# Causal mask of transposed attention scores: one 128x128 matmul per head in place of two 64x64 ones

## The chip, the cores and the metric
The kernel runs on one core of one Trainium2 chip. The metric is device time in microseconds (us) of one execution. Lower is better. TensorE, the matrix engine, appears in the profile as PE (matmuls) and PEld (loading of the stationary operand). VectorE is DVE, ScalarE is ACT, GpSimd is POOL and SyncE, which issues transfers, is SP.

## The reference, cut to what matters
The network has two layers. The first is a state space mixer with a dense mixture of experts, the second is causal self-attention with a routed mixture of experts. The change lies in the attention of the second layer, which has 4 sequences of 512 tokens, 16 heads, and 8 numbers per head:

```
q = apply_rope((x @ W_q.T).reshape(B, S, H, dk).transpose(0, 2, 1, 3))
k = apply_rope((x @ W_k.T).reshape(B, S, H, dk).transpose(0, 2, 1, 3))
v = (x @ W_v.T).reshape(B, S, H, dk).transpose(0, 2, 1, 3)
scores = jnp.einsum('bhqd,bhkd->bhqk', q, k) / sqrt(dk)
scores = jnp.where(jnp.tril(jnp.ones((S, S), dtype=bool)), scores, -jnp.inf)
probs = jax.nn.softmax(scores, axis=-1)
attn = jnp.einsum('bhqk,bhkd->bhqd', probs, v)
```

A query sees only keys at its own position or before it. Of each 128x128 tile on the diagonal, the half with keys behind the query is masked.

## The kernel before, in words
Attention is done in 16 groups of four heads: group s is sequence b = s // 4, heads 4(s % 4) to 4(s % 4) + 3. One pass of the loop `for it in range(-2, 17)` (line 1719) handles three groups at different stages, in eight slots i = 0 to 7. The order of TensorE's work is written out by hand in this loop, and the other engines have loops of the same form. In one slot TensorE does:

- `scores(it + 2, u)` (line 1628, its matmul is recorded under L1641): scores of the group two ahead with queries as rows, into one of three PSUM banks that are used in turn (`RING = 3`, function `ring_bank`). DVE takes the maximum of each row from there (L1221) and so frees the bank. A head's operand has 48 rows (q and k each split in bf16 pieces) and lies in partitions 0 to 47 or 64 to 111, by the head's parity. Slots 0, 2 and 4 hold work of an even head alone, 1, 3 and 5 of an odd head alone, 6 and 7 of both.
- `scores_T(8 * it + i)` (line 1655): one unit of transposed scores of the present group, keys as rows, for two heads, hh = 0 in partitions 0 to 63 and hh = 1 in partitions 64 to 127. First the mask is written to the unit's two banks (L1667), then the scores are accumulated over it (L1672, 51 rows: 48 and three that subtract the row's maximum). It waits for `probs` of the unit two before. The key tile is 3 for slots 0 and 1, then 2, 1 and 0, so that the score matmul has 128, 256, 384 and 512 columns.
- In odd slots `weighted_values` (L1686, fp32, output of 32 columns per head), which waits for `probs`; in slot 2 `maxima_T` (L1651); in slot 3 `o_T` (L1695); in some passes `a_T` (L1702), `attn_out` (L1710), projections of q and k (L1599) and of v (L1624).

ACT computes the exponentials of a unit from its two banks (`probs`, L778). POOL splits the finished maxima in bf16 pieces (`max_parts`, L522 to L528) before `maxima_T` can transpose them. There are 128 units in all. Passes it = 14 and 15 have no `scores`.

In the listings a matmul's shape is written rows*columns of the stationary operand, then that of the moving one: `64*128 64x64` is 64 rows and 128 output partitions with 64 columns streamed.

The mask operand comes from `shape_constants` and is loaded once, in the bf16 constant pack.

Of the kernel before, what the change touches and what calls it, by code (L numbers as in the profile page):

```python
# [13 lines left out]
P = 128  # L14
# [14 lines left out]
HALF = 64  # L29
# [4 lines left out]
NEG = -1e30  # L34
# [19 lines left out]
    "const": [("ident", 128), ("tri", 128), ("after", 128), ("cos", 512), ("sin", 512), ("iota", 8),  # L54
              ("mask", 512), ("segment", NT * E1), ("full", NT), ("block", NBLK), ("number", NT), ("spare", NBLK)],
}
BPACK = [("identb", 128), ("causal", 256), ("half", 64)]


def offsets(fields):  # L60
    out, at = {}, 0
    for name, width in fields:
        out[name] = (at, at + width)
        at += width
    return out, at


def adaln_kernel(nc, x_in, mod_in, mixw_in, moe0_in, attn_in, moe1_in, const_in, bconst_in, kones_in, out):
    with ExitStack() as ctx:
        def sb(name, shape, dt=F32):  # L70
            return ctx.enter_context(nc.sbuf_tensor(name, shape, dt))
# [3 lines left out]
        def sem(name):  # L75
            if name not in sems:
                sems[name] = ctx.enter_context(nc.semaphore(name))
            return sems[name]

        ps = ctx.enter_context(nc.psum_tensor("ps", [P, 8, 512], F32))  # L80

        w = {}
        packed = {}
        for pack, fields in PACKS.items():
# [4 lines left out]
            for name, (lo, hi) in off.items():  # L89
                w[name] = t[:, lo:hi]  # L90
        off, total = offsets(BPACK)
        bconst = sb("bconst", [P, total], BF16)
        for name, (lo, hi) in off.items():
            w[name] = bconst[:, lo:hi]
        ident, identb = w["ident"], w["identb"]
# [1241 lines left out]
        def _(pe):  # L1337
            pe.wait_ge(sem("siluc"), 1)
            for c in range(6):
                for layer in range(2):  # L1340
                    mm = pe.matmul(ps[:, 0, (2 * c + layer) * B:(2 * c + layer + 1) * B],
                                   w[f"wmod{layer}"][:, c * D:(c + 1) * D], siluc[:, layer * B:(layer + 1) * B],
                                   start=True, stop=True)
# [4 lines left out]
            for b in range(B):  # L1348
                for n, c in enumerate((0, 1, 2)):
                    mm = pe.matmul(ps[:, 1 + b, n * D:(n + 1) * D], modT[:, c, 0, b:b + 1].to_broadcast([P, P]), ident,  # L1350
                                   start=True, stop=True)
                mm.then_inc(sem("mod0_ps"), 1)
            for b in range(B):
                if b == 3:
                    pe.wait_ge(sem("mod0"), 1)
                for n, c in enumerate((2, 3, 4, 5)):
                    mm = pe.matmul(ps[:, MOD1_BANK[b], n * D:(n + 1) * D], modT[:, c, 1, b:b + 1].to_broadcast([P, P]),
                                   ident, start=True, stop=True)
# [69 lines left out]
            for i in range(NT + 3):  # L1428
                if i < NT:

                    t, k = i, i % 2
                    tok = slice(t * P, (t + 1) * P)
                    pe.wait_ge(sem("ua"), HEADS * (t + 1))
                    if t >= 2:
                        pe.wait_ge(sem("L"), t - 1)
                    pe.matmul(ps[:, k, :], w["after"], ua[:, k].rearrange("p h s -> p (h s)"), start=True,
                              stop=True).then_inc(sem("seg_ps"), 1)
                    if t >= 1:
# [3 lines left out]
                              stop=True).then_inc(sem("g_ps"), 1)  # L1442
                if i < 2:
                    to_tokens(B - 2 + i)
                if 0 <= i - 2 < NT:
                    t, k = i - 2, i % 2
# [9 lines left out]
                if 0 <= i - 1 < NT:  # L1456

                    t, k = i - 1, (i - 1) % 2
                    c, b = t % TPB, t // TPB
                    tok = slice(t * P, (t + 1) * P)  # L1460
                    if c < TPB - 1:
                        pe.wait_ge(sem("Xd"), t + 1)
                        if t >= 1:
                            pe.wait_ge(sem("prev"), 3 * b + c)
                        pe.matmul(ps[:, 5, k * DI:(k + 1) * DI], Bt[:, t, :], Xd[:, k].rearrange("p h e -> p (h e)"),
                                  start=True, stop=True).then_inc(sem("state_ps"), 1)
# [11 lines left out]
                    for hh in range(HEADS):  # L1478
                        mm = pe.matmul(ps[:, 3 + k, hh * HP:(hh + 1) * HP], M[:, k, hh, :], X[:, k, hh, :],
                                       start=True, stop=True)  # L1480
                    mm.then_inc(sem("y_ps"), 1)
                if 0 <= i - 3:
                    t, k = i - 3, (i - 3) % 2
# [6 lines left out]
                    for q in range(2):  # L1490
                        mm = pe.matmul(ps[:, 7, P * (1 + k):P * (2 + k)], yT[:, k, q, :], wor[:, q, :],
                                       start=(q == 0), stop=(q == 1))
# [80 lines left out]
            for i in range(32):  # L1573
                e = i % E0
                pe.wait_ge(sem("xm"), i + 1)
                if i >= 2:
# [3 lines left out]
                          stop=True).then_inc(sem("p1_ps"), 1)  # L1580
                pe.matmul(ps[:, 4 + i % 2, :], w["w3"][:, e * D:(e + 1) * D], xm[:, i % 2, :], start=True,  # L1581
                          stop=True).then_inc(sem("p3_ps"), 1)
# [72 lines left out]
            def scores_T(u):  # L1655
                s, i = divmod(u, 8)
                b, g = divmod(s, QG)
                kt, jp = 3 - i // 2, i % 2
                n = S - kt * P
                if i == 0:  # L1660
                    pe.wait_ge(sem(f"m_rows{s % 2}"), 64 * (s // 2 + 1))
                if u >= 2:
                    pe.wait_ge(sem("probs"), u - 1)
                for qh in range(2):
                    for hh in range(2):
                        bank, lo = 4 + 2 * (u % 2) + hh, HALF * hh
                        pe.matmul(ps[:, bank, HALF * qh:HALF * (qh + 1)],  # L1667
                                  w["causal"][lo:lo + HALF, qh * P:(qh + 1) * P], w["half"][lo:lo + HALF, :],
                                  start=(qh == 0), stop=True, skip_group_check=True)
                for hh in range(2):  # L1670
                    bank, lo = 4 + 2 * (u % 2) + hh, HALF * hh
                    mm = pe.matmul(ps[:, bank, 0:n], kaug[lo:lo + KM, b % 2, 2 * g + jp, kt * P:(kt + 1) * P],  # L1672
                                   qaug[lo:lo + KM, b % 2, 2 * g + jp, kt * P:S], start=False, stop=True,
                                   skip_group_check=True)
                mm.then_inc(sem("st_ps"), 1)
# [43 lines left out]
            for it in range(-2, 17):  # L1719
                if it == -1:  # L1720
                    transposes(3, 2, bank=4)
                    transposes(3, 3, bank=4)
                for i in range(8):
                    if it + 2 < 16:
                        for u in at_slot[i]:
                            scores(it + 2, u)
                    if 0 <= it < 16:
                        scores_T(8 * it + i)
                    if i % 2 == 1 and 0 <= 4 * it + i // 2 - 1 < 64:
                        weighted_values(4 * it + i // 2 - 1)  # L1730
                    if i == 2 and 0 <= it + 1 < 16:
                        maxima_T(it + 1)
                    if i == 3 and 0 <= it - 1:
                        o_T(it - 1)
                    if i == 5 and it >= 4 and it % 4 == 0:
                        a_T(it // 4 - 1)
                    if i == 7 and it >= 4 and it % 4 == 0:
                        attn_out(it // 4 - 1)
                    for b, j in ropes_at(it, i):
                        project(b, j)  # L1740
                    if it in (4, 8) and i == 6:
                        project_values((it + 4) // 4)
# [45 lines left out]
def shape_constants():  # L1788
    import numpy as np

    k = np.arange(P)
    pos = np.arange(S, dtype=np.float32)
    inv = np.float32(10000.0) ** (-np.arange(0, DK, 2, dtype=np.float32) / np.float32(DK))
    ang = (pos[:, None] * inv[None, :]).astype(np.float32)
    d = np.arange(P) % DK
    cos = np.cos(ang)[:, d // 2].T
    sin = np.sin(ang)[:, d // 2].T * np.where(d % 2 == 0, -1.0, 1.0)[:, None]
    mask = np.zeros((P, 4 * P), np.float32)
    mask[:, 3 * P:4 * P] = np.where(k[None, :] > k[:, None], NEG, 0.0)
    const = {  # L1800
        "ident": np.eye(P), "tri": k[:, None] <= k[None, :], "after": k[:, None] > k[None, :],
        "cos": cos, "sin": sin, "iota": np.broadcast_to(8.0 - np.arange(8), (P, 8)), "mask": mask,
        "segment": np.broadcast_to(np.arange(NT * E1) % NT > 0, (P, NT * E1)),
        "full": np.broadcast_to(P * np.arange(NT), (P, NT)),
        "block": np.broadcast_to(np.arange(NBLK), (P, NBLK)),
        "number": 1 + k[:, None] + P * np.arange(NT)[None, :],
        "spare": 1 + NTOK + k[:, None] + P * np.arange(NBLK)[None, :],
    }
    bconst = {
        "identb": np.eye(P),  # L1810
        "causal": np.concatenate([np.where(k[None, :] > k[:, None] % HALF + HALF * qh, NEG, 0.0) for qh in range(2)],
                                 axis=1),
        "half": k[:, None] % HALF == np.arange(HALF)[None, :],
    }
    fc = np.concatenate([np.asarray(const[n], np.float32) for n, _ in PACKS["const"]], axis=1)
    bc = np.concatenate([np.asarray(bconst[n], np.float32) for n, _ in BPACK], axis=1).astype(np.dtype("bfloat16"))
    kones = np.full((3, NH // 2, S), -1.0, np.float32)
    return fc, bc, kones.astype(np.dtype("bfloat16"))


def lay_out(i):
# [41 lines left out]
    }  # L1863
    packs["x_in"] = np.ascontiguousarray(a["L0_attn_x"].reshape(NT, P, D).transpose(1, 0, 2))
    packs["const_in"], packs["bconst_in"], packs["kones_in"] = shape_constants()
    return packs

# [14 lines left out]
```

## Time and profile before

| | |
|---|---|
| median of 3 timed runs | 580.0 us (579.58 to 580.09) |
| the profiled execution's own time | 577.07 us |
| its span in the trace | 575.2 us |
| mean granted TensorE clock | 0.889 of full |
| PE busy, DVE busy, ACT busy, POOL busy | 452.4, 392.0, 278.1, 271.6 us |
| attention loop, from the first L1667 to the last | 313.9 to 460.2 us |
| L1667, the mask matmuls | 512 matmuls, 45.6 us busy, 195 ns mean |
| L1672, the transposed scores | 256 matmuls, 52.2 us busy, 307 ns mean |

A span is the time from the first to the last instruction in the trace. The 1.9 us between it and the execution's own time lie around it. Busy time of an engine is the union of its instructions' durations. The duration of a matmul includes its way through the array, which overlaps with the next matmul. So what a matmul costs in a stream is the distance from its start to the start of the next, not its duration.

### The profile page before, as it was taken

The numbers are of one execution on the slowest core, as the hardware profiler recorded it, in microseconds if no ns is written. First come the engines' busy times: TensorE is split into PE (matmuls) and PEld (weight loads), VectorE is DVE, ScalarE is ACT, GpSimd is POOL, SyncE is SP. The second block draws the span as 40 slices with busy tenths as digits, with TensorE's granted clock in tenths as the row PEclk, the third lists the DMA queues.
The fourth block names the chain that finished last, engine by engine and source line by source line (L and its number), as shares of the span: only waits on it lengthen the run. The fifth ranks groups of instructions, "written<-read, shape, count | busy, mean of one in ns | idle before, by whom it ended". The sixth has DMA issues, their size and how long they took to land.

```text
span 575.2 us, 10088 instructions
## 1 busy us (share of the span) xinstructions
PE 452.4 (79%) x3120; PEld 274.4 (48%) x3120; DVE 392.0 (68%) x1264; ACT 278.1 (48%) x518; POOL 271.6 (47%) x392
## 2 busy tenths in 40 slices
PE   3688778987998999994558998999999863059970
PEld 3545456766653444442323434435445343049970
DVE  5789738988655888886679687888898235025533
ACT  1568796653453544441223577678777831013220
POOL 4210038998301786664641047476655502714541
PEclk9988889999799999997775799999999985559995
DMA  8600000000335333310386012222300000141114
GB/s 354 169 1 1 0 2 2 1 2 1 144 148 125 99 106 99 107 62 2 108 208 124 4 31 88 82 86 85 84 5 4 3 0 10 52 123 36 36 38 146
DMA packets 25739, 39.94 MB, mean 69 GB/s; under 512 B 3228, under 2 KB 17756, under 8 KB 25164
## 3 DMA queue, kind: packets, MB, share of 16 engines
q1 hardware_dynamic: 21752, 30.42, 17.8%
q0 software_dynamic: 3936, 8.89, 5.2%
q8 instruction: 26, 0.43, 0.3%
q14 instruction: 25, 0.20, 0.1%
HBM read 27.55 MB, written 11.55 MB: 68 GB/s over the span
## 4 chain that ended last, share of the span: by engine, by line
PE 49%; DVE 18%; POOL 11%; issue 8%; ACT 6%; DMA 6%; SPq 0%; DVEq 0%; POOLq 0%; ACTq 0%
PE ps L1579 5%; PE ps L1581 5%; PE ps L1568 5%; PE ps L1686 4%; PE ps L1599 3%; PE ps L1771 3%; PE ps L1782 3%; POOL slots_x L586 3%; DVE rows L406 3%; PE ps L1391 2%; DVE moe L1221 2%; PE ps L1641 2%; POOL qk_parts L305 2%; DVE st L387 2%; PE ps L1672 2%
## 5 line engine op out<-in xcount | busy, mean ns | idle before, releaser
L1221 DVE CUSTOM_DVE_ANT_0 moe<-ps,const 128x512 bf16<-128x512 f32 (+3 forms) x256 | 110.5, 486 | 9.7 <-PE ps L1641 9.4
L778 ACT ACTIVATE arena<-ps 128x256 f32<-128x256 f32 (+3 forms) x128 | 85.8, 701 | 33.6 <-PE ps L1672 32.9
L476 POOL TENSOR_TENSOR arena<-arena 128x512 f32<-128x512 f32 x32 | 51.7, 1616 | 51.9 <-DVE arena L1139 51.7
L1641 PE MATMUL ps<-arena 48*128 48x128 bf16 (+3 forms) x256 | 56.1, 329 | 10.7 <-DVE arena L1221 4.7
L1672 PE MATMUL ps<-arena 51*128 51x128 bf16 (+3 forms) x256 | 52.2, 307 | 0.0
L1686 PE MATMUL ps<-arena 128*32 128x512 f32 (+3 forms) x512 | 48.4, 450 | 0.9 <-ACT arena L778 0.6
L1667 PE MATMUL ps<-bconst 64*128 64x64 bf16 x512 | 45.6, 195 | 1.2 <-ACT arena L778 0.5
L1641 PEld LDWEIGHTS ps<-arena 48*128 48x128 bf16 x256 | 16.7, 97 | 55.7 <-DVE arena L1221 31.7
L751 ACT ACTIVATE arena<-arena 128x512 f32<-128x512 f32 x32 | 20.2, 630 | 41.9 <-DVE arena L1139 41.6
L838 ACT ACTIVATE arena<-ps 128x512 f32<-128x512 f32 x23 | 13.7, 597 | 55.0 <-PE ps L1771 55.0
L592 POOL DMA_INDIRECT tokens_y<-arena,token_at x23 | 22.1, 960 | 32.5 <-DVE arena L1325 31.3
L950 DVE SCALAR_TENSOR_TENSOR arena<-ps,mixw,arena 128x511 f32<-128x511 f32 (+2 forms) x48 | 33.1, 737 | 5.2 <-ACT arena L643 5.2
L1667 PEld LDWEIGHTS ps<-bconst 64*128 64x128 bf16 x512 | 29.5, 97 | 12.0 <-ACT arena L778 4.5
L1579 PE MATMUL ps<-arena,moe 128*128 128x512 f32 x64 | 32.8, 593 | 1.8 <-DVE arena L1122 1.8
L441 POOL TENSOR_TENSOR arena<-arena 128x256 f32<-128x256 f32 x16 | 12.4, 776 | 44.4 <-DVE arena L933 40.5
L1581 PE MATMUL ps<-arena,moe 128*128 128x512 f32 x64 | 32.7, 592 | 0.0
L1568 PE MATMUL ps<-arena,moe 128*128 128x512 f32 x64 | 32.5, 592 | 0.0
L1130 DVE SCALAR_TENSOR_TENSOR arena<-ps,moe,arena 128x512 f32<-128x512 f32 x32 | 24.0, 751 | 12.3 <-PE ps L1581 12.2
L1762 PE MATMUL ps<-const,arena 128*128 128x128 f32 x23 | 6.5, 293 | 29.1 <-DMA arena<-slots_x 29.1
L1367 PE MATMUL ps<-const,rows 128*128 128x128 f32 x64 | 13.8, 367 | 17.6 <-DVE rows L406 14.9
L1771 PE MATMUL ps<-arena 128*128 128x128 f32 x184 | 26.5, 290 | 0.6 <-DVE arena L1321 0.5
L1139 DVE SCALAR_TENSOR_TENSOR arena<-ps,moe,arena 128x512 f32<-128x512 f32 x32 | 24.0, 751 | 3.5
(239 smaller groups left out, 1113.2 us busy)
## 6 DMA issues: line engine op xcount, KB each, us to landing
arena<-expert_weights SPq DMA_DIRECT2D x32, 256.0 KB, 3.2
arena<-moe_in SPq DMA_DIRECT2D x1, 4100.0 KB, 12.8
qk_parts<-arena SPq DMA_DIRECT2D x24, 128.0 KB, 2.3
qk_parts<-arena POOLq DMA_DIRECT2D x24, 128.0 KB, 2.3
arena<-qk_parts POOLq DMA_DIRECT2D x32, 96.0 KB, 2.5
arena<-qk_parts SPq DMA_DIRECT2D x8, 288.0 KB, 5.6
moe<-moe_in SPq DMA_DIRECT2D x1, 1936.0 KB, 13.8
slots_x<-zeros SPq DMA_DIRECT2D x1, 1518.0 KB, 19.6
```

The source lines that it names most:

```text
L476: pool.tensor_tensor(yacc[:, ts], yacc[:, ts], pr[:, i % 2, :], ALU.add).then_inc(sem("yacc"), 1)
L778: act.activation(pt[:, u % 4, :, 0:n], ps[:, 4 + 2 * k:6 + 2 * k, 0:n], ACT.Exp, scale=ATT_SCALE).then_inc(sem("probs"), 1)
L950: v.scalar_tensor_tensor(out=acc[b % 2][:, c, s:S], in0=ps[:, c, 0:S - s], scalar=w["conv_w"][:, 4 * c + 3 - s:4 * c + 4 - s], in1=acc[b % ...
L1221: v.tensor_tensor_reduce(out=junk[:, done % 2, 0:n], in0=ps[:, k, col:col + n], in1=w["mask"][:, (3 - qt) * P:4 * P], scale=1.0, scalar=3 ...
L1568: pe.matmul(ps[:, 6 + i % 2, :], w["w2"][:, e * D:(e + 1) * D], gT[:, i % 2, :], start=True, stop=True).then_inc(sem("p2_ps"), 1)
L1579: pe.matmul(ps[:, 2 + i % 2, :], w["w1"][:, e * D:(e + 1) * D], xm[:, i % 2, :], start=True, stop=True).then_inc(sem("p1_ps"), 1)
L1581: pe.matmul(ps[:, 4 + i % 2, :], w["w3"][:, e * D:(e + 1) * D], xm[:, i % 2, :], start=True, stop=True).then_inc(sem("p3_ps"), 1)
L1641: mm = pe.matmul(ps[:, k, col:col + n], qaug[lo:lo + KR, b % 2, 2 * g + j // 2, qt * P:(qt + 1) * P], kaug[lo:lo + KR, b % 2, 2 * g + j // ...
L1667: pe.matmul(ps[:, bank, HALF * qh:HALF * (qh + 1)], w["causal"][lo:lo + HALF, qh * P:(qh + 1) * P], w["half"][lo:lo + HALF, :], start=(qh ...
L1672: mm = pe.matmul(ps[:, bank, 0:n], kaug[lo:lo + KM, b % 2, 2 * g + jp, kt * P:(kt + 1) * P], qaug[lo:lo + KM, b % 2, 2 * g + jp, kt * P:S] ...
L1686: mm = pe.matmul(ps[32 * j:32 * j + 32, 3, kt * P:S], va[:, b % 2, kt, 4 * (s % QG) + j, :], pt[:, (2 * m + j // 2) % 4, j % 2, 0:n], star ...
L1771: mm = pe.matmul(ps[:, j % 2, q * P:(q + 1) * P], w1[:, j % 2, q * P:(q + 1) * P], xT[:, j % 2, :], start=True, stop=True)
```

## The change
For each unit the four mask matmuls (two halves of the queries for each of two heads, each with the 64 partitions of its head) become two (one per head), each with all 128 partitions of a 128x128 mask and the 128x128 identity as moving operand. The written values are the same. The constant pack loses 192 of its 448 bf16 columns.

```
-BPACK = [("identb", 128), ("causal", 256), ("half", 64)]
+BPACK = [("identb", 128), ("causal", 128)]
...
-                for qh in range(2):
-                    for hh in range(2):
-                        bank, lo = 4 + 2 * (u % 2) + hh, HALF * hh
-                        pe.matmul(ps[:, bank, HALF * qh:HALF * (qh + 1)],
-                                  w["causal"][lo:lo + HALF, qh * P:(qh + 1) * P], w["half"][lo:lo + HALF, :],
-                                  start=(qh == 0), stop=True, skip_group_check=True)
+                for hh in range(2):
+                    pe.matmul(ps[:, 4 + 2 * (u % 2) + hh, 0:P], w["causal"], identb, start=True, stop=True,
+                              skip_group_check=True)
...
-        "causal": np.concatenate([np.where(k[None, :] > k[:, None] % HALF + HALF * qh, NEG, 0.0) for qh in range(2)],
-                                 axis=1),
-        "half": k[:, None] % HALF == np.arange(HALF)[None, :],
+        "causal": np.where(k[None, :] > k[:, None], NEG, 0.0),
```

## Rows read from the trace of the kernel before
**Rows 1.** The page: busy time by engine, and the chain that ended last by engine.
```profile
PE 452.4 (79%) x3120; PEld 274.4 (48%) x3120; DVE 392.0 (68%) x1264; ACT 278.1 (48%) x518; POOL 271.6 (47%) x392
...
PE 49%; DVE 18%; POOL 11%; issue 8%; ACT 6%; DMA 6%; SPq 0%; DVEq 0%; POOLq 0%; ACTq 0%
```
**Rows 2.** Stretches: us, then PE, PEld, DVE, ACT, POOL busy (instructions), clock, DMA share, GB/s.
```profile
314.00:323.00 9.00, 8.77 (x75) 4.00 (x75) 5.43 (x25) 4.06 (x7) 0.87 (x4) 0.50 0.01 3
...
420.00:430.00 10.00, 9.51 (x124) 4.36 (x122) 9.39 (x43) 7.95 (x13) 4.08 (x7) 1.00 0.01 3
314.00:461.00 147.00, 138.13 (x1683) 66.15 (x1683) 114.43 (x517) 105.50 (x171) 78.59 (x152) 0.96 0.16 46
450.00:462.00 12.00, 10.07 (x148) 3.87 (x145) 1.10 (x4) 10.63 (x17) 6.68 (x7) 1.00 0.01 2
```
**Rows 3.** Groups of PE matmuls, 314 to 461 us: busy us, mean ns; idle before, releaser.
```profile
L1641 PE MATMUL ps<-arena 48*128 48x128 bf16 (+3 forms) x223 | 45.5, 311 | 3.9 <-DVE arena L1221 3.0 <-DVE moe L1156 0.7
...
L1651 PE MATMUL ps<-bconst,arena 128*12 128x128 bf16 x60 | 6.0, 225 | 3.3 <-POOL arena L528 3.3
```
**Rows 4.** Timeline of PE, slots 0 and 1 of pass 11: start, length, us.
```profile
422.04 0.39 PE L1641 MATMUL ps<-arena 48*128 48x512 bf16 x1
422.05 0.23 PE L1667 MATMUL ps<-bconst 64*128 64x64 bf16 x2
422.11 0.22 PE L1672 MATMUL ps<-arena 51*128 51x128 bf16 x1
422.18 0.38 PE L1641 MATMUL ps<-arena 48*128 48x512 bf16 x1
422.27 0.22 PE L1667 MATMUL ps<-bconst 64*128 64x64 bf16 x2
422.33 0.22 PE L1672 MATMUL ps<-arena 51*128 51x128 bf16 x1
422.44 0.23 PE L1667 MATMUL ps<-bconst 64*128 64x64 bf16 x4
422.51 0.22 PE L1672 MATMUL ps<-arena 51*128 51x128 bf16 x2
422.66 1.06 PE L1686 MATMUL ps<-arena 128*32 128x512 f32 x8
```
**Rows 5.** Timeline of PE, slots 2 to 4 of pass 11.
```profile
423.66 0.33 PE L1641 MATMUL ps<-arena 48*128 48x384 bf16 x1
...
423.95 0.27 PE L1672 MATMUL ps<-arena 51*128 51x256 bf16 x1
424.15 0.39 PE L1651 MATMUL ps<-bconst,arena 128*12 128x128 bf16 x4
424.47 0.33 PE L1641 MATMUL ps<-arena 48*128 48x384 bf16 x1
...
424.96 0.43 PE L1686 MATMUL ps<-arena 128*32 128x128 f32 x8
425.31 0.66 PE L1695 MATMUL ps<-const,mod 128*128 128x128 f32 x4
425.90 0.28 PE L1641 MATMUL ps<-arena 48*128 48x256 bf16 x1
```
**Rows 6.** Timeline of PE, from slot 5 of pass 11 to slot 0 of pass 12.
```profile
426.74 0.64 PE L1686 MATMUL ps<-arena 128*32 128x256 f32 x8
427.31 0.41 PE L1641 MATMUL ps<-arena 48*128 48x512 bf16 x2
...
427.60 0.40 PE L1672 MATMUL ps<-arena 51*128 51x512 bf16 x2
428.02 0.39 PE L1641 MATMUL ps<-arena 48*128 48x384 bf16 x2
428.63 0.33 PE L1641 MATMUL ps<-arena 48*128 48x384 bf16 x1 [0.22 <-DVE arena L1221]
...
429.23 0.85 PE L1686 MATMUL ps<-arena 128*32 128x384 f32 x8
430.01 0.39 PE L1641 MATMUL ps<-arena 48*128 48x512 bf16 x1
```
**Rows 7.** Timeline of PE in pass 0.
```profile
316.92 0.40 PE L1672 MATMUL ps<-arena 51*128 51x256 bf16 x1
317.24 0.65 PE L1686 MATMUL ps<-arena 128*32 128x128 f32 x8
```

## The prediction
> **What bounds the kernel now.** I read the page first: PE has the most busy time and the largest share of the chain that ended last, 49% [rows 1]. The change touches only the attention loop, so next come the stretches of that loop. From 314 to 461 us PE is busy 138.1 of 147.0 us, DVE 114.4, ACT 105.5 [rows 2]. Busy PE is a modelled number, so I went to the single starts in the timeline of a quiet pass, number 11, which runs from 422.04 to 430.01, 7.97 us [rows 4, 6]. The reader is to see that nearly every PE start there follows the one before at the distance that its columns need, and that real waits stand in slots 6 and 7 alone, where `scores` waits for DVE to free one of three banks. In that stretch DVE is busy 9.39 of 10 us and PE 9.51 [rows 2]. So PE sets the pace, with DVE close behind: time added to PE in slots 0 to 5 goes to the span, time added in slots 6 and 7 meets a wait.
>
> **What a matmul costs now.** Distances between starts, at full clock:
> - Columns: the four L1651 matmuls, 128 columns each, take 0.39 us from first start to last end, and one lasts 0.22, so three steps are 0.17: 56 ns for 128 columns [rows 5]. 64 columns then are about 29 ns, 256 are 110, 384 are 162, 512 are 216.
> - The mask: four L1667 start at 422.44, the two L1672 at 422.51. That is about 70 ns (two steps, 39 and 29), since the matmul of hh = 0 and that of hh = 1 stream side by side in their own halves of the rows [rows 4].
> - Side by side also across slots: at 422.05 the mask of hh = 1 runs while a 512-column score matmul occupies the rows of hh = 0, and at 422.18 slot 1's scores start beside slot 0's unfinished unit [rows 4].
> - Change of shape: where the stationary shape goes from 51 rows to 128x32, the next start comes 0.15 us after one of 128 columns (422.51 to 422.66), 94 ns more than its columns [rows 4]. From 512 columns it is 429.23 - 428.92, 0.31 us against 0.216, the same 94 (428.92 is slot 7's last L1672: 428.63, then 162 + 56 ns of scores, 39 and 29 of mask). From 128x12 to 48 rows: 424.47 less the last L1651 start at 424.32 is 0.15, again 94. From 128x128 (L1695) to 48 rows: last start 425.31 + 0.66 - 0.27 = 425.70, next 425.90, 0.20 us where its own step is 0.11: 90 [rows 5]. I find no change of this kind without the gap, so I take 95 ns each way. The exact case, 48 or 51 rows to 128x128 in bf16 and back, is not in the trace. Its bounds are 0 (if the gap belongs to the fp32 and 32-column shapes) and 150 ns (95 plus the 56 by which the first of four L1695 steps, 0.66 - 0.27 - 2 x 0.11 = 0.17, exceeds the others, a load that isn't hidden). I take 95, since four different pairs agree on it.
>
> The Trainium skill, TensorEngine Tiling (Array Packing), section Key Properties, says that changing the tiling mode, not just the tile, drains TensorE. By it each unit here pays two drains, and the sum below is what it gives; the rows above agree, with their 90 to 94 ns. The same skill, Perfetto Trace Analysis, section Matmuls, says that larger matmuls are more efficient than smaller ones when possible. By it alone the change should gain, and that is the last rival below.
>
> **The change, slot by slot (pass 11).** A unit's mask becomes two steps of 56 ns in place of 70, and a change of shape stands before and behind it: 42 + 190 = 0.23 us. Nothing can stream beside a 128-row matmul, so what now overlaps is lost too.
> - Slots 0 and 1: now 422.04 to 422.66, 0.62 us. After: scores 216, gap 95, mask 112, gap 95, then slot 0's L1672 and, in the rows of hh = 1 behind it, slot 1's scores, 56 + 216, gap 95, mask 112, gap 95, L1672 56, and the present gap of 94 to L1686: 1.24. +0.62.
> - Slot 2: now 423.66 to 424.15, 0.49. After: 162 + 56 + 95 + 112 + 95 + 110 + 94 = 0.72. +0.23. Slot 3, 424.47 to 424.96, the same.
> - Slots 4 and 5: now 425.90 to 426.74, 0.84. After: 2 x 110 + 95 + 112 + 95 = 0.52, L1672 162, scores 2 x 110, 95 + 112 + 95, L1672 162, 94: 1.46. +0.62.
> - Slots 6 and 7: now 427.31 to 429.23, 1.92, of which streams need 1.09 (216 + 68 + 216, then 218 + 68 + 216 + 94); the rest is the wait for banks and what it pulls out of step. After, the streams need 1.57. DVE comes to slot 6 without backlog, since slots 0 to 5 last longer. It needs about 0.27 us from the scores' start plus 0.62 for a 512-column maximum, and the fourth bank of the two slots is wanted 0.74 after slot 6 starts, so one score pair still starts about 0.2 late: 1.79. -0.13 in place of the +0.48 that the streams would give.
>
> **The sum.** Passes 1 to 13: 13 x (0.62 + 0.23 + 0.23 + 0.62) = 22.1. Slots 6 and 7: I count 11 passes of them with that wait, 11 x -0.13, and two where a projection of v leaves none, 2 x 0.48: -0.5. L1651 waits 3.3 us in all for POOL's pieces of the maxima [rows 3]; those depend on DVE's maxima from slot 7 and on POOL's queue, and slot 2 comes 0.85 us later than now, so nearly all of it goes: -3.2. Pass 0 runs at the half clock, 0.50, PE's lower level of 1.2 GHz, after a stretch in which PE waited [rows 2]. There the gap from L1672 is 0.32 us less 213 ns for 256 columns, 0.11 [rows 7], and the streams take twice as long: about 0.35 for each of seven units and 2 x 0.3 of lost overlap, +3.1. Passes 14 and 15 have no scores, so a unit already stands behind a change of shape in half the slots: 1.4 a pass, 2.7; ACT, busy 10.63 of 12 us there, paces the end [rows 2], and I take 1.5. Other work: the smaller constant pack is loaded long before and beside larger loads, 0; no DMA, wait or queue entry is moved on SP, POOL or ACT. What is late next is PE itself. Together 22.1 - 0.5 - 3.2 + 3.1 + 1.5 = 23.0. Against the profiled execution: 577.1 + 23.0 = 600.1. The median of the timed runs lies 2.9 above that execution, so 603.0.
>
> The ends: with no wait absorbed the streams add 13 x 2.2 + 3.1 + 2.7 = 34.4, 614. With every real idle of PE in the loop absorbed, an estimated 1 us a pass (0.6 in pass 11, more where L1651 waits), 18.4, 598.
>
> **The rivals.**
> 1. *The gap isn't there between bf16 shapes.* Then a unit costs 42 ns and the lost overlap stays (about 0.15 in each of slots 0/1 and 4/5): 0.64 a pass, 14 x 0.64 = 9, less some 2 of L1651's wait, about +7: 587. For it: no row has the exact pair. Against: the gap is the same for bf16 and fp32, 32 and 128 columns, in both directions.
> 2. *A weight load that isn't hidden.* The second mask matmul waits for its 128-row load, 56 ns as in the first step of L1695 [rows 5]: 128 x 0.056 = 7.2, 610.
> 3. *DVE is the bound and takes PE's addition.* For it: 9.39 of 10 us [rows 2]. Then nothing to 0.2% changes, 580. Against: slots 0 to 5 have no wait of PE at all, and DVE is busy 114 of 147 in the whole loop.
> 4. *Faster.* One mechanism: a small mask matmul is paid by the instruction and not by the column. If the two steps (39 and 29 ns) are instruction costs, the change leaves one such step fewer per unit, 30 to 39 ns at the mask, 128 x 0.035 = 4.5 us: 575.5. It decides if the two new mask matmuls and the gaps around them take under 70 ns together. Against: L1651's steps of 56 ns for 128 columns already cost 112 for two, and the gaps would have to be absent.
>
> **How the numbers follow.** Forecast 0.78 (its own range 596 to 612), rival 1 0.07, rival 2 0.10, rival 3 0.03, rival 4 0.02. What a measurement can tell here is about 0.2%, 1.2 us. Slower: 0.78 + 0.07 + 0.10 = 0.95; same 0.03; faster 0.02. The range leaves out rivals 3 and 4, most of 1, and the far ends: 592 to 614.
>
> **What would show it.** In the trace after, the quiet pass 11 should last 9.5 us in place of 7.97. In each unit the two L1667 (128*128 128x128) start 56 ns apart, about 95 ns behind the columns of what stood before, and L1672 starts 0.15 after the second. L1641 of slot 1 no longer starts before slot 0's L1672. L1651's idle time is near 0 and L1641's wait for L1221 much smaller; the loop from the first L1667 to the last is about 169 us instead of 146. DVE's share in the loop falls under 0.7. I am wrong if the mask-to-score distance is near 56 ns (rival 1), if the two mask starts are over 100 ns apart (rival 2), or if slots 6 and 7 grow by the full 0.48 because DVE's pace and PE's no longer meet, which would put the time above 610.

## The result: 27 us slower, and the profile after

| | before | after |
|---|---|---|
| median of timed runs | 579.79 us (577.23 to 580.09, 4 runs) | 606.43 us (604.10 to 608.49, 4 runs) |
| ratio after/before | | 1.0469 (95% interval 1.0420 to 1.0517) |
| profiled execution, its span | 577.07, 575.2 us | 608.49, 606.7 us |
| attention loop, first to last start of the transposed scores | 146.2 us | 171.1 us |
| mean granted clock | 0.889 | 0.887 |

Before the loop the two traces differ by about 5 us, after it by 1.3 us. Nothing there is changed but the size of one load, and further below a second trace of the changed kernel shows that most of the 5 us is spread. The loop's 25 us is the change's.

First the page of the changed kernel, busy time by engine and the chain that ended last, against [rows 1]. Then its stretches, against [rows 2]: the loop's start, a quiet 10 us, the whole loop, the end of the loop.

```profile
PE 489.8 (81%) x2864; PEld 278.3 (46%) x2864; DVE 393.6 (65%) x1264; ACT 282.8 (47%) x518; POOL 271.2 (45%) x392
...
PE 63%; DVE 16%; issue 6%; ACT 6%; POOL 5%; DMA 4%; SPq 0%; DVEq 0%; POOLq 0%; ACTq 0%
```
```profile
318.00:327.00 9.00, 8.58 (x54) 2.71 (x53) 5.64 (x28) 3.94 (x7) 0.87 (x4) 0.50 0.01 3
440.00:450.00 10.00, 9.96 (x90) 3.83 (x90) 7.50 (x34) 6.62 (x11) 4.74 (x8) 1.00 0.01 3
318.00:491.00 173.00, 170.96 (x1424) 67.28 (x1427) 116.49 (x521) 109.72 (x170) 78.21 (x152) 0.97 0.14 39
480.00:491.00 11.00, 10.72 (x108) 4.41 (x106) 1.10 (x4) 8.87 (x14) 5.45 (x6) 1.00 0.00 1
```

PE issues 256 matmuls fewer and takes a larger share of the chain, 63% against 49%. In the quiet stretch DVE's busy time went from 9.39 to 7.50 of 10 us: the same work is spread over a longer pass, and DVE waits for PE's scores in between.

The timeline of PE in the changed kernel, slots 0 to 4 of pass 11 (start, length), against [rows 4, 5]:

```profile
445.31 0.39 PE L1641 MATMUL ps<-arena 48*128 48x512 bf16 x1
445.63 0.28 PE L1665 MATMUL ps<-bconst 128*128 128x128 bf16 x2
445.85 0.23 PE L1669 MATMUL ps<-arena 51*128 51x128 bf16 x2
445.92 0.38 PE L1641 MATMUL ps<-arena 48*128 48x512 bf16 x1
446.23 0.28 PE L1665 MATMUL ps<-bconst 128*128 128x128 bf16 x2
446.44 0.23 PE L1669 MATMUL ps<-arena 51*128 51x128 bf16 x2
446.60 1.07 PE L1683 MATMUL ps<-arena 128*32 128x512 f32 x8
447.60 0.39 PE L1641 MATMUL ps<-arena 48*128 48x384 bf16 x2
447.92 0.28 PE L1665 MATMUL ps<-bconst 128*128 128x128 bf16 x2
448.14 0.28 PE L1669 MATMUL ps<-arena 51*128 51x256 bf16 x2
448.35 0.39 PE L1651 MATMUL ps<-bconst,arena 128*12 128x128 bf16 x4
448.67 0.39 PE L1641 MATMUL ps<-arena 48*128 48x384 bf16 x2
...
449.43 0.43 PE L1683 MATMUL ps<-arena 128*32 128x128 f32 x8
449.78 0.66 PE L1692 MATMUL ps<-const,mod 128*128 128x128 f32 x4
450.37 0.39 PE L1641 MATMUL ps<-arena 48*128 48x256 bf16 x2
```

The reader is to see three things. From the 512-column scores at 445.31 the mask starts 0.32 us later, 0.10 more than the columns need (0.216). The mask's two matmuls start 0.066 us apart by the single starts in the trace (0.28 from the first start to the last end, of which the second lasts 0.22), and the scores start 0.22 after the first, that is 0.154 after the second, 0.10 more than its 56 ns. So one unit pays 0.10 + 0.066 + 0.056 + 0.10 = 0.32 us where it paid 0.07. And slot 1's scores (445.92) start behind slot 0's unit, where they started beside it before (422.18 in [rows 4]). What the 0.10 us consists of, no run takes apart. The weight load of the new shape is recorded to start with its matmul (445.62) and not ahead of it, while that of the second mask matmul starts 55 ns ahead.

Slots 5 to 7 of the same pass, and the waits of two groups in the loop (idle time before them), against [rows 6] and [rows 3]:

```profile
451.88 0.64 PE L1683 MATMUL ps<-arena 128*32 128x256 f32 x8
452.45 0.39 PE L1641 MATMUL ps<-arena 48*128 48x512 bf16 x2
452.77 0.28 PE L1665 MATMUL ps<-bconst 128*128 128x128 bf16 x2
452.99 0.39 PE L1669 MATMUL ps<-arena 51*128 51x512 bf16 x2
453.22 0.80 PE L1641 MATMUL ps<-arena 48*128 48x384 bf16 x4
453.95 0.28 PE L1665 MATMUL ps<-bconst 128*128 128x128 bf16 x2
454.17 0.39 PE L1669 MATMUL ps<-arena 51*128 51x512 bf16 x2
454.49 0.85 PE L1683 MATMUL ps<-arena 128*32 128x384 f32 x8
```
```profile
L1641 PE MATMUL ps<-arena 48*128 48x384 bf16 (+2 forms) x224 | 49.4, 308 | 1.4 <-DVE arena L1221 1.1
...
L1651 PE MATMUL ps<-bconst,arena 128*12 128x128 bf16 x60 | 6.0, 225 | 0.0
```

Pass 11 is not typical: of the passes without other work (3, 7, 9, 10 and 11) it is the one in which the kernel before waits least. Each of these lasts 9.97 us after the change, but 9.10, 9.04, 8.40, 8.44 and 7.97 before. Over passes 1 to 13 the growth is 1.68 us on average, from 0.87 in pass 3 to 2.14 in pass 12. In pass 3 of the kernel before PE stood still ahead of L1651, for POOL, and the change fills that wait instead of adding to it:

```profile
348.19 0.39 PE L1651 MATMUL ps<-bconst,arena 128*12 128x128 bf16 x4 [1.06 <-POOL arena L528]
```

### The profile page after: what moved, and what is told of

Same layout as the page of the kernel before. It is cut to its first block, busy times and chain, and to the rows that moved or that the text cites. A ratio compares the mean times of both kernels' runs of the same rounds, so it can differ in the third digit from the quotient of the medians.

```text
span 606.7 us, 9576 instructions
## 1 busy us (share of the span) xinstructions
PE 489.8 (81%) x2864; PEld 278.3 (46%) x2864; DVE 393.6 (65%) x1264; ACT 282.8 (47%) x518; POOL 271.2 (45%) x392
## 4 chain that ended last, share of the span: by engine, by line
PE 63%; DVE 16%; issue 6%; ACT 6%; POOL 5%; DMA 4%; SPq 0%; DVEq 0%; POOLq 0%; ACTq 0%
PE ps L1683 7%; PE ps L1641 6%; PE ps L1669 5%; PE ps L1579 5%; PE ps L1568 5%; PE ps L1581 5%; PE ps L1665 4%; PE ps L1599 3%; PE ps L1768 3%; PE ps L1779 3%; DVE rows L406 3%; POOL slots_x L586 2%; PE ps L1391 2%; DVE st L387 2%; PE ps L1692 2%
## 5 line engine op out<-in xcount | busy, mean ns | idle before, releaser
L778 ACT ACTIVATE arena<-ps 128x256 f32<-128x256 f32 (+3 forms) x128 | 88.0, 703 | 54.9 <-PE ps L1669 52.7
L1641 PE MATMUL ps<-arena 48*128 48x128 bf16 (+3 forms) x256 | 59.3, 324 | 8.1 <-ACT arena L786 4.3
L1641 PEld LDWEIGHTS ps<-arena 48*128 48x128 bf16 x256 | 17.1, 96 | 51.9 <-DVE arena L1221 23.4
L1669 PE MATMUL ps<-arena 51*128 51x128 bf16 (+3 forms) x256 | 40.3, 312 | 0.0
L1665 PE MATMUL ps<-bconst 128*128 128x128 bf16 x256 | 37.1, 228 | 0.7 <-DMA arena<-arena 0.4
L1130 DVE SCALAR_TENSOR_TENSOR arena<-ps,moe,arena 128x512 f32<-128x512 f32 x32 | 24.0, 751 | 12.1 <-PE ps L1581 12.0
L1665 PEld LDWEIGHTS ps<-bconst 128*128 128x128 bf16 x256 | 14.8, 97 | 32.0 <-issue 25.6
L522 POOL CAST arena<-arena 128x16 bf16<-128x16 f32 x16 | 3.4, 215 | 56.1 <-DVE arena L1221 56.1
```

Of the source, the lines that this page charges most:

```text
L778: act.activation(pt[:, u % 4, :, 0:n], ps[:, 4 + 2 * k:6 + 2 * k, 0:n], ACT.Exp, scale=ATT_SCALE).then_inc(sem("probs"), 1)
L1641: mm = pe.matmul(ps[:, k, col:col + n], qaug[lo:lo + KR, b % 2, 2 * g + j // 2, qt * P:(qt + 1) * P], kaug[lo:lo + KR, b % 2, 2 * g + j // ...
L1665: pe.matmul(ps[:, 4 + 2 * (u % 2) + hh, 0:P], w["causal"], identb, start=True, stop=True, skip_group_check=True)
```

## The experiments
Times are medians, ratios are against the kernel before on the same chip. "Loop" is the distance from the first to the last start of the transposed scores, in the one trace of each run. TensorE's clock rises from the half to the full level near the loop's start, 9.8 to 10.7 us behind it in most traces, 6.1 to 6.6 us in those of e3, e7, e8, e9 and e11, 13.4 in e4. Pass 0 is shorter or longer by that (11.56 us before, 9.97 in e7), so the last column leaves it out.

| run | median us | ratio, 95% interval | loop us | passes 1 to 15, us |
|---|---|---|---|---|
| before | 578.5 to 579.8 in the sets of runs | | 146.2 | 134.6 |
| changed | 606.4 | 1.0469 (1.0420 to 1.0517) | 171.1 | 157.5 |
| e1 one column of 128 rows | 599.67 | 1.0346 (1.0297 to 1.0396) | 165.8 | 152.7 |
| e2 one column of 64 rows | 581.79 | 1.0047 (1.0022 to 1.0073) | 147.8 | 135.8 |
| e3 changed, no mask | 577.26 | 0.9975 (0.9940 to 1.0011) | 144.1 | 134.6 |
| e4 changed, mask twice | 619.04 | 1.0687 (1.0639 to 1.0736) | 184.4 | 169.1 |
| e5 masks of two units per visit | 599.57 | 1.0362 (1.0313 to 1.0412) | 165.1 | 152.1 |
| e6 changed, heads side by side | 595.26 | 1.0309 (1.0255 to 1.0363) | 160.6 | 148.2 |
| e7 before, maxima beside values | 575.37 | 0.9936 (0.9909 to 0.9963) | 141.5 | 131.6 |
| e8 before, heads side by side | 577.09 | 0.9962 (0.9932 to 0.9992) | 143.5 | 133.3 |
| e9 e7 and e8 together | 575.10 | 0.9931 (0.9906 to 0.9955) | 141.2 | 131.1 |
| e10 changed, once more | 604.67 | 1.0452 (1.0416 to 1.0487) | 171.2 | 157.5 |
| e11 e5 and e6 together | 592.20 | 1.0239 (1.0193 to 1.0285) | 156.4 | 145.6 |

**e1: the change of shape alone, and e2: its control.** Ahead of the old four mask matmuls:

```
+                pe.matmul(ps[:, 4 + 2 * (u % 2), 0:1], identb, identb[:, 0:1], start=True, stop=True,
+                          skip_group_check=True)
```
In e2 the operands are `identb[0:HALF, :]` and `identb[0:HALF, 0:1]`.

> The kernel before, with its four 64-row mask matmuls, and ahead of them in each unit one matmul of a 128x128 bf16 stationary operand with a single column, whose result the mask overwrites. It adds two changes of shape per unit and next to no columns. Shape theory (a visit to a 128-row operand costs a gap of about 95 ns each way, and nothing streams beside it): nearly the whole loss of the change comes back, some 215 ns a unit and 0.3 us of lost overlap a pass, less the waits absorbed: 602 to 608 us. Column theory (the loss is the columns and the weight loads of the 128x128 mask): one more small matmul, at most 30 ns a unit, 580 to 584 us.

> The control to the one-column 128-row matmul: the same single column, but with a 64-row stationary operand, so that no shape changes. Shape theory: 30 ns a unit at most, partly beside the other half of the rows, 579 to 584 us. If any extra matmul or weight load in a unit costs much whatever its shape (instruction theory), this run is as slow as the one with 128 rows, above 600 us.

Measured: one column with a 128-row operand costs 19.6 us of loop and 3.5% of the kernel's time; one column with a 64-row operand 1.6 us and 0.5%. The difference, 18.0 us of the change's 24.9, is from the change of shape and what it stops from running side by side, not from the number of matmuls. e1 came 2.3 us faster than the lower bound that was expected. The timeline of e1, slots 0 and 1 of a pass, has the gaps and the lost overlap:

```profile
440.00 0.39 PE L1641 MATMUL ps<-arena 48*128 48x512 bf16 x1
440.32 0.18 PE L1664 MATMUL ps<-bconst 128*128 128x1 bf16 x1
440.43 0.23 PE L1669 MATMUL ps<-bconst 64*128 64x64 bf16 x4
440.50 0.22 PE L1674 MATMUL ps<-arena 51*128 51x128 bf16 x2
440.56 0.38 PE L1641 MATMUL ps<-arena 48*128 48x512 bf16 x1
440.87 0.18 PE L1664 MATMUL ps<-bconst 128*128 128x1 bf16 x1
```

The one column starts 0.32 after 512 columns, as the full mask does, and the 64-row mask follows it by 0.11 us.

**e3: no mask.** The mask matmuls of the changed kernel are left out and the scores start with `start=True`; this kernel leaves out the causal mask of the transposed scores and computes something else.

> The changed kernel without any mask matmul; the first score matmul starts the accumulation instead (the causal mask of the transposed scores is left out). It is the floor of both kernels. Shape theory: the changed kernel's mask costs all its loss and what the old mask cost, so this lies below the kernel before by what its 70 ns a unit cost, 9 us at most and less where PE then waits for DVE: 572 to 578 us. If something else of the change (the smaller constant pack, another place in memory) made the loss, this run stays above 590 us.

Measured: not to be told from the kernel before, its interval holds 1. So of the old mask's 9 us of PE time (70 ns in each of 128 units) hardly anything comes back, since PE then waits more for others. The loop of 144.1 us alone is no fair measure of that, for this trace has the full clock early in pass 0 and a second stretch at the half clock in pass 3 (11.00 us for 9.10; the clock is the third number from the end):

```profile
354.00:358.00 4.00, 4.00 (x24) 1.10 (x26) 3.38 (x15) 3.35 (x5) 3.99 (x7) 0.50 0.37 105
```

In the 13 passes that neither touches (all but 0, 3 and 4) 7.3 us of mask steps are gone, and the time falls by 1.3 us. The idle times of PE's groups in e3's loop show the longer waits, above all for POOL's pieces of the maxima (for DVE and POOL it was 3.0 and 3.3 us in [rows 3]):

```profile
L1641 PE MATMUL ps<-arena 48*128 48x384 bf16 (+3 forms) x226 | 45.5, 317 | 4.9 <-DVE arena L1221 3.1 <-DVE moe L1156 1.2
...
L1651 PE MATMUL ps<-bconst,arena 128*12 128x128 bf16 x60 | 6.0, 225 | 5.3 <-POOL arena L528 5.3
```

It also shows that nothing else in the change (a smaller constant pack, other addresses) makes the loss.

**e4: the mask twice.** `for hh in (0, 1, 0, 1):` in the changed kernel.

> The changed kernel with each 128x128 mask matmul issued twice, the second over the first: the columns and weight loads double, the changes of shape stay. Shape theory: two more steps of 56 to 66 ns per unit, 128 x 0.11 to 0.13 = 14 to 17 us more than the changed kernel's 606, less a little wait: 619 to 624 us. Column theory (the mask's own streams and loads are the whole loss of 27 us over the kernel before): another 27 us and more, 633 us.

Measured: 13.3 us more loop than the changed kernel, 104 ns a unit. By the single starts the third and the fourth mask matmul take 56 ns each, their columns, so 112 ns a unit, and their weight loads are hidden. Pass 11 grew by 0.78 us, which is seven units of 0.112: slot 6's falls into the wait for a bank that is there anyway. The loss of 24.9 us is not the mask's own streams.

**e5: masks of two units in one visit.**

```
+                if u % 2 == 0:
+                    if u >= 2:
+                        pe.wait_ge(sem("probs"), u)
+                    for bank in range(4, 8):
+                        pe.matmul(ps[:, bank, 0:P], w["causal"], identb, start=True, stop=True,
+                                  skip_group_check=True)
```

> The changed kernel with the 128x128 masks of two units written in one visit: in even slots four mask matmuls (this unit's banks and the next one's), in odd slots none. The visit then waits for the exponential of the unit just before, not of the one before that. The streams are the same, only half the visits to the 128-row shape are left. Shape theory: 64 x 0.19 = 12 us less than the changed kernel, 594 to 597 us, pass 11 at about 9.2 us instead of 9.97; the new wait costs under 0.1 us, since that exponential ends before the visit in all slots by the trace. Column theory: the same columns, so 606 us, or more by the new wait.

Measured: 6.0 us less loop instead of 12. The gaps halve, but I was wrong on the new wait: PE stood still 9.6 us for exponentials in this loop (0.3 in the changed kernel), 0.9 us of it in pass 11, which lasted 9.75 us for 9.2 expected. The timeline of e5 in slots 6 and 0 has it at the visit, for the exponentials of slots 5 and 7:

```profile
440.66 0.39 PE L1641 MATMUL ps<-arena 48*128 48x512 bf16 x2
441.38 0.40 PE L1666 MATMUL ps<-bconst 128*128 128x128 bf16 x4 [0.33 <-ACT arena L778]
...
443.25 0.39 PE L1641 MATMUL ps<-arena 48*128 48x512 bf16 x1
444.23 0.38 PE L1666 MATMUL ps<-bconst 128*128 128x128 bf16 x4 [0.58 <-ACT arena L778]
```

I had judged the exponentials by the changed kernel's slots. That the odd slots, now without a visit, leave ACT less time before the next one is my reading; no run took it apart.

**e6 and e8: row scores of even and odd heads in the same slot**, in the changed kernel and in the one before.

```
-            [[(3, 0)]],
-            [[(3, 1)]],
-            [[(2, 0), (0, 0)]],
-            [[(2, 1), (0, 1)]],
-            [[(1, 0), (1, 2)]],
-            [[(1, 1), (1, 3)]],
+            [[(3, 0)], [(3, 1)]],
+            [],
+            [[(2, 0), (0, 0)], [(2, 1), (0, 1)]],
+            [],
+            [[(1, 0), (1, 2)], [(1, 1), (1, 3)]],
+            [],
```

> The changed kernel with the row scores put in other slots: those of the even and of the odd heads together in slots 0, 2 and 4, where they can stream side by side in the two halves of the rows, and none in slots 1, 3 and 5. Lost-overlap theory: the changed kernel streams them one after the other because a 128-row visit stands between; together they take 0.22 us less in each of three slot pairs, 14 x 0.65 = 9 us, less what the pairs then wait for a bank: 598 to 603 us. If lost overlap is no part of the loss, 606 us or more by the waits for banks.

> The kernel before, its 64-row masks kept, with the same regrouping of the row scores as in the run of the changed kernel. Lost-overlap theory: here slots 0 with 1 and 4 with 5 overlap already, only slots 2 with 3 can gain, 14 x 0.2 = 3 us at most, and the three banks then stall PE more often: between 2 us faster and 6 us slower. The regrouping should thus gain clearly less here than on the changed kernel.

Measured: 10.5 us less loop on the changed kernel (1.4 to 1.6 points of the ratio, 8 to 9 us), 2.7 us on the old one (0.4 points, 2.2 us). Of the 2.7 us, 1.4 lie in pass 0, where the full clock came 4 us earlier in e8's trace. In passes 1 to 15 the regrouping is worth 9.3 us on the changed kernel and 1.3 us on the old one, so it is worth far more where a visit to 128 rows stands between the two heads' scores. The lost overlap is real. But not all of the gain is the overlap that the change lost. Pass 11 is 0.74 us shorter: 0.21 in slots 0 and 1, 0.21 in slots 4 and 5, and 0.32 in slots 2 and 3. The part of slots 2 and 3 holds 0.22 us of overlap that the old kernel didn't have either, for L1651 stands between them, and 0.10 us for one change of shape fewer, since the mask of slot 3 now follows L1651 without 48-row scores between. The timeline of e6, slots 2 and 3:

```profile
435.33 0.40 PE L1641 MATMUL ps<-arena 48*128 48x384 bf16 x4
435.66 0.28 PE L1665 MATMUL ps<-bconst 128*128 128x128 bf16 x2
435.88 0.28 PE L1669 MATMUL ps<-arena 51*128 51x256 bf16 x2
436.09 0.39 PE L1651 MATMUL ps<-bconst,arena 128*12 128x128 bf16 x4
436.41 0.29 PE L1665 MATMUL ps<-bconst 128*128 128x128 bf16 x2
```

At 595.3 us e6 is below my range of 598 to 603.

**e7: transposes of the maxima moved beside the weighted values**, in the kernel before: `if i == 2` becomes `if i == 3` for `maxima_T`, for ACT's copy and for the entry in the order of the banks.

> The kernel before with the transposes of the maxima moved from slot 2 to slot 3, right behind the weighted values (ACT's copy of them moved along). Both have 32-column output, so two changes of shape fewer per pass. If PE were the only bound, 16 x 0.19 = 3.0 us less than before. The kernel without a mask showed that PE time taken out of this loop returns only in part, since DVE is close behind: I expect 0.5 to 2.5 us less. If changes of shape are free where DVE paces, no difference.

Measured: 0.64% or 3.7 us, more than I expected, and 4.7 us of loop. 1.6 us of the loop's gain are likely not the change's: pass 0 lasts 9.97 in place of 11.56 us, and the full clock came about 6.6 us after the loop's start at 316.8 in this execution, 10.5 in that of before. Stretches of e7, the clock is the third number from the end:

```profile
321.00:323.00 2.00, 2.00 (x11) 0.70 (x10) 0.82 (x6) 1.30 (x2) 0.00 (x0) 0.50 0.01 3
323.00:325.00 2.00, 1.81 (x12) 0.35 (x10) 1.08 (x2) 0.48 (x1) 0.00 (x0) 0.91 0.01 3
```

The rest, 3.1 us, equals the 3.0 of two gaps in 16 passes by chance, for it is a sum of several things: single passes went from 1.01 us shorter (pass 4) to 0.48 us longer (pass 14). The regrouping does more than take out two gaps. With L1651 gone from between slots 2 and 3, their scores run side by side as well, and the way from slot 2's scores to slot 4's fell from 2.24 to 1.97 us, of which two gaps are 0.19. POOL also has one slot more for its pieces: the wait of L1651 fell from 3.3 to 0.8, while that of L1641 for DVE rose from 3.0 to 4.8. How much of the gain each of the three made, no run shows.

**e9: both on the kernel before.**

> The kernel before with both regroupings: transposes of the maxima beside the weighted values (alone 3.7 us faster) and the row scores of even and odd heads side by side (alone 2.2 us faster). If both take PE time from the same place, where DVE then paces, together 4 to 5 us, 574.5 to 576; if they add, 6 us, 573.5 us. Both need PE to be the bound in part of the loop; the loop should last 140 us or a little less, and pass 11 near 7.6 us.

Measured: 575.1, no better than e7 alone. They don't add, and the loop of 141.2 us is longer than the 140 expected. Both stand about 4 us below the kernel before; single executions overlap with its own, but both intervals of the ratio leave 1 out. e7 with three edited conditions is the version to keep.

**e10: the changed kernel once more, and e11: e5 and e6 together.**

> The changed kernel once more, for its ratio against the kernel before in the same hour and for a second trace. 604 to 607 us. In the first trace the attention loop began 4.8 us later than in the trace of before, although nothing ahead of it is changed but the size of one load. If that is a spread of single executions (other stretches at the half clock), this trace's loop begins somewhere between 314 and 320 us and still lasts 171 us; if it belongs to the change, it begins at about 319 again.

> The changed kernel with masks written for two units in one visit (alone 6.9 us faster) and the scores of even and odd heads side by side (alone 9 to 11 us faster). Half the visits and no lost overlap: what is left of the loss should be the 64 visits with their gaps, 12 us, the columns, some 6 us, less what DVE's pace hides, plus the wait for the exponential of the unit before: 588 to 592 us. If it is at 580 the 128-row mask has no price of its own left.

Measured: e10's loop again lasts 171.2 us, pass 11 again 9.97, but it begins at 316.0 us instead of 318.9. The start moves from one execution to the next (314.0 to 319.6 in all traces here), and so does the clock ahead of it (0.91 on average over the first 100 us in the trace of before, 0.86 in the first one of the changed kernel). So the 5 us before the loop is not shown to be the change's. e11 is 592.2, at the upper end of my range: even with half the visits and no lost overlap the kernel with the 128-row mask is 2.4% slower than the old one.

## Why the prediction was right
It said 603.0 us, range 592 to 614, slower; measured 606.4 and 604.7. By its steps:

1. *PE sets the pace, DVE is close behind.* Right, and they are closer than I told: e3 takes 9 us of PE time out of the loop and returns nothing measurable, while of the 34.4 us of streams that the prediction counted, the loop paid 24.9. One way the loop is bound by PE, the other way by DVE, POOL and ACT. And "PE sets the pace" was read from pass 11, where PE waits 0.22 us; in pass 3 it waits 1.3 us, and there the change cost 0.87 us and not 2.0. The prediction has this in its term for L1651, not in its picture of the loop.
2. *95 ns for each change of shape, for the exact pair too.* Right: 0.10 and 0.10 us, in both traces of the changed kernel and in e1. The bounds of 0 and 150 ns were both far. This settles rival 1 (no gap between bf16 shapes). At the half clock, in pass 0, the gap at the mask is 0.14 us (0.24 from the start of a 128-column matmul, whose columns take 0.11), where the prediction took 0.11. The Trainium skill, TensorEngine Tiling (Array Packing), section Key Properties, says that a change of the tiling mode drains TensorE; the trace agrees, with 0.10 us at each of them.
3. *56 ns for each mask matmul.* 66 and 56. The second takes 10 ns more than its columns, not 56: rival 2 falls, and e4 shows 56 ns for each further one.
4. *Lost overlap between slots.* Right: slot 1's scores start after slot 0's unit. e6 against e8 shows the price.
5. *Slots.* Slots 0 and 1 took 1.29 us (445.31 to 446.60; forecast 1.24), slot 2 0.75 (0.72), slot 3 0.76 (0.72), slots 4 and 5 1.51 (450.37 to 451.88; 1.46). The excess of 0.03 a unit, 0.17 a pass, is the 10 ns of step 3 and gaps of 100 instead of 95.
6. *Slots 6 and 7: 1.79.* This is the term that was mis-sized: 2.04 us (452.45 to 454.49), +0.12 in place of -0.13. I gave the first bank's way 0.27 us from the scores' start to DVE's, and 0.62. The timeline of DVE in the changed kernel, at a slot 6 whose scores start at 442.49:

```profile
442.91 0.69 DVE L1221 CUSTOM_DVE_ANT_0 moe<-ps,const 128x512 bf16<-128x512 f32 x1 [0.45 <-PE ps L1641]
443.53 0.08 DVE L1221 DVE_READ_ACCUMULATOR2_ANT arena<- 128x1 f32 x1
```

DVE starts 0.42 after the scores, that is just behind their recorded end (0.39) and not behind their columns (0.22). It then takes 0.62, and the scores that need the bank start 0.14 later, after the accumulator's read: 1.18 after slot 6's in place of 0.89. 0.25 us in each of 11 passes is 2.7 us, more than the 1.9 us by which the sum was short.
7. *L1651's wait goes, 3.2 us.* Right: 0.0 after.
8. *Passes 0, 14 and 15.* 2.1 us for +3.1, and 1.0 for +1.5: both too dear.
9. *The sum.* +23.0 forecast, +24.9 of loop measured, +25.4 to +26.6 in the medians. Passes 1 to 13 gave +21.9 for a forecast 18.4, the others +3.1 for 4.6. That the sum came so near is in part luck: slots 0 to 5 were 2.2 us too cheap (0.17 in 13 passes) and slots 6 and 7 2.7 us, against 1.5 us too dear in passes 0, 14 and 15, and the longer waits of the kernel before in passes other than 11, which the change filled, took up the rest. Pass 11 alone was forecast to grow by 1.57 us and grew by 2.0.

Rival 3 (DVE hides it) and rival 4 (fewer matmuls gain) fall: pass 11 went from 7.97 to 9.97 us, and e2 puts the price of one more small matmul in the same shape at 13 ns of loop a unit. The other rule weighed there (the Trainium skill, Perfetto Trace Analysis, section Matmuls: larger matmuls are more efficient than smaller ones, when possible) doesn't hold where the larger one changes the shape: half the matmuls, each with twice the rows and columns, took 2.0 us more in pass 11.

## What to carry to other kernels
Before small matmuls are merged into a large one, look at what stands before and behind them on TensorE. If these use half of the rows, the merged one costs two changes of shape, 0.1 us each here, and ends whatever ran side by side; 0.07 us became 0.32. Put operations of one shape next to each other, and judge a saving on an engine by what waits for the others: here 9 us of mask gave back next to nothing, while moving four small transposes by one slot gave 3.7 us.

## What the runs showed that I had not expected
- Removing all mask matmuls gained no measurable time (ratio 0.9975, 0.9940 to 1.0011), while moving four small transposes by one slot gained 0.64%. What PE time is worth depends on who makes PE wait next.
- The changed kernel is slower but more regular: five passes that lasted 7.97 to 9.10 us all last 9.97, since the waits that made them differ are filled.
- A single column with a 128-row operand costs nearly as much as the whole 128x128 mask: 19.6 of 24.9 us of loop.
- DVE starts 0.42 us after the start of the 512-column matmul that it waits for, whose columns take 0.22, and with three banks in turn that latency is paid once a pass.
